# A transformer block with linear attention on one core: the loop over 13 of 17 positions replaced by straight code on all five engines

## The reference

```python
x_norm = (x - mu) * rsqrt(var + EPS) * ln_g + ln_b
q, k, v = split(x_norm @ W_qkv + b_qkv)
gate = sigmoid(x @ W_gate + b_gate); gate = gate / (mean(gate) + EPS)
q = relu(q * gate) ** 2 + EPS;  k = relu(k * gate) ** 2 + EPS
# scan over the rows: kv_s += k_t (x) v_t ; k_s += k_t ; out_t = (q_t . kv_s) / (q_t . k_s + EPS)
x = x + out @ W_proj + b_proj
# feed-forward, on the layer norm of the new x
x = x + gelu((x_n @ U1) @ V1 + b1) @ U2 @ V2 + b2
```

## Time and profile before

| | |
|---|---|
| time, median of 3 runs | 1889.18 us (1887.97 to 1893.83) |
| the profiled execution's own time | 1888.3 us |
| its span, first to last instruction | 1886.3 us |
| mean granted TensorE clock | 0.991 of 2.4 GHz |
| PE busy | 1813.1 us, 96% |
| DVE, POOL, ACT busy | 75%, 47%, 36% |
| instructions recorded | 37376 |

### The profile page before, as it was taken

The page is one execution under the profiler, slowest core; times in us unless marked ns, Lnnn a source line. Parts: engine busy times, 40 slices in busy tenths (PEclk is TensorE's granted clock), DMA queues, the critical chain, the costliest instruction groups (busy, mean ns, idle before and its releaser), DMA issues.

```text
span 1886.3 us, 37376 instructions
## 1 busy us (share of the span) xinstructions
PE 1813.1 (96%) x13753; PEld 1545.6 (82%) x13753; DVE 1407.7 (75%) x2606; ACT 683.7 (36%) x1242; POOL 881.2 (47%) x1091
## 2 busy tenths in 40 slices
PE   6899999999999999999999999999999999999997
PEld 4688888888888888888888888888888888888876
DVE  6777777777777777777777777777777677777775
ACT  4233343343343333333333433433433333333332
POOL 3354554454544545545545444545544455455440
PEclk9999999999999999999999999999999999999999
DMA  6101001001000011010011010010100110100000
GB/s 195 34 18 34 28 31 35 22 25 35 25 33 24 24 35 34 23 35 23 24 34 35 23 34 24 23 35 25 33 24 28 30 34 23 35 23 24 29 18 23
DMA packets 34501, 61.20 MB, mean 32 GB/s; under 512 B 3672, under 2 KB 6256, under 8 KB 34352
## 3 DMA queue, kind: packets, MB, share of 16 engines
q1 hardware_dynamic: 33488, 57.31, 9.6%
q10 hardware_dynamic: 864, 1.57, 0.3%
HBM read 41.96 MB, written 16.91 MB: 31 GB/s over the span
## 4 chain that ended last, share of the span: by engine, by line
issue 36%; POOL 25%; PE 18%; ACT 4%; DVE 3%; POOLq 1%; DVEq 0%
POOL h_lo L372 9%; POOL xs L361 4%; POOL keys L389 3%; POOL small L334 3%; POOL queries L392 2%; PE ps_a L773 2%; PE ps_a L772 2%; PE ps_a L774 2%; POOL key_lo L401 2%; POOL x1s L382 2%; PE ps_b L774 2%; PE ps_b L773 2%; PE ps_b L772 2%; ACT L471 2%; PE ps_q L772 1%
## 5 line engine op out<-in xcount | busy, mean ns | idle before, releaser
L372 POOL TENSOR_TENSOR h_lo<-h_full,h_hi 128x512 fp32r<-128x512 f32 x244 | 313.9, 1286 | 382.8 <-DVE h_hi L602 382.8
L456 ACT ACTIVATE h_full<-ps_h,cols 128x256 f32<-128x256 f32 x512 | 211.1, 472 | 242.7 <-PE ps_h L774 235.2
L602 DVE CAST h_hi<-h_full 128x512 fp32r<-128x512 f32 x256 | 163.6, 639 | 98.8 <-ACT h_full L456 98.7
L772 PE MATMUL ps_b<-wx_hi,zt_hi 128*128 128x512 f32 x512 | 209.7, 410 | 22.7 <-issue 21.5
L334 POOL TENSOR_TENSOR small<-moments,eps_col 128x1 f32<-128x1 f32 x128 | 25.8, 201 | 399.7 <-DVE moments L741 331.7
L772 PE MATMUL ps_a<-wx_hi,zt_hi 128*128 128x512 f32 x512 | 207.2, 405 | 1.3 <-issue 1.2
L774 PE MATMUL ps_b<-wx_hi,zt_lo 128*128 128x512 f32 x512 | 205.4, 401 | 0.0
L773 PE MATMUL ps_b<-wx_lo,zt_hi 128*128 128x512 f32 x512 | 205.3, 401 | 0.0
L774 PE MATMUL ps_a<-wx_hi,zt_lo 128*128 128x512 f32 x512 | 202.2, 395 | 0.0
L773 PE MATMUL ps_a<-wx_lo,zt_hi 128*128 128x512 f32 x512 | 201.8, 394 | 0.0
L772 PE MATMUL ps_q<-h_hi,u_hi 128*128 128x256 f32 x512 | 162.4, 317 | 15.3 <-POOL h_lo L372 9.2
(11 more groups left out here) (160 smaller groups left out, 5052.1 us busy)
## 6 DMA issues: line engine op xcount, KB each, us to landing
xs<-L_attn_x SPq DMA_DIRECT2D x64, 256.0 KB, 2.7
out<-x1s SPq DMA_DIRECT2D x64, 256.0 KB, 2.1
key_sums<-carry_rows SPq DMA_DIRECT2D x60, 256.0 KB, 3.2
x1s<-L_attn_W_qkv SPq DMA_DIRECT2D x8, 256.0 KB, 5.2
x1s<-L_attn_W_gate SPq DMA_DIRECT2D x4, 256.0 KB, 4.0
h_full<-L_attn_W_qkv SPq DMA_DIRECT2D x4, 256.0 KB, 6.3
x1s<-L_ffn_U SPq DMA_DIRECT2D x4, 256.0 KB, 3.6
carry_rows<-key_sums SPq DMA_DIRECT2D x64, 2.0 KB
```

Source lines behind the costliest of these rows:

```text
L372: E.tensor_tensor(h_lo[:, i % 2, :], h_full[:, i % 2, :], h_hi[:, i % 2, :].bitcast(F32), ALU.subtract).then_inc(s["h_lo_ready"], 1)
L456: last = E.activation(h_full[:, i % 2, a * GROUP:(a + 1) * GROUP], ps_h[i % 2][:, a * GROUP:(a + 1) * GROUP], ACT.Gelu_apprx_tanh, bias=b1 ...
L602: E.tensor_copy(h_hi[:, i % 2, :], h_full[:, i % 2, :]).then_inc(s["h_hi_ready"], 1)
L772: E.matmul(ps, wh, mh, start=start and i == 0, stop=False)
```

## The change

The helper steps loses the hardware loop. All 17 positions with their four steps are written out, so p is always a number: the branches are gone from each engine, and with them the register instructions; each wait gets a constant and each DMA a constant row. Order, waits, buffers and the work of a step stay as they are.

```diff
-def steps(eng, step):
-
-    for p in (0, 1):
-        for b in range(4):
-            step(p, b)
-    with eng.Fori(2, POSITIONS - 1) as p:
-        for b in range(4):
-            step(p, b)
-    for p in (POSITIONS - 1, POSITIONS):
-        for b in range(4):
+def steps(step):
+
+    for p in range(POSITIONS + 1):
+        for b in range(BATCHES):
             step(p, b)
...
-            steps(sp, step)
+            steps(step)
...
-            steps(pool, step)
+            steps(step)
...
-            steps(act, step)
+            steps(step)
...
-            steps(dve, step)
+            steps(step)
...
-            steps(pe, step)
+            steps(step)
```

## The result

| | before | after |
|---|---|---|
| time, median of 4 runs | 1888.58 us (1887.96 to 1893.83) | 1856.32 us (1854.23 to 1857.23) |
| ratio, 95% interval | | 0.982 (0.980 to 0.984) |
| the profiled execution | 1888.3 us | 1856.7 us |
| its span | 1886.3 us | 1854.6 us |

The change saves 32 us, 1.8%. The forecast was 1856.0. After it six lines fewer stand at the top, so L772 is now L766, L372 is L366, and L625 is L619.

What follows compares the result with a forecast made beforehand. PE bounds the kernel, held up at its loop's twelve jumps. Span 1886.3 less 32.9 (idle 22.7, restart 3.4, clock 6.2, small shifts 0.6) gives 1853.4, execution 1855.4, raised towards the median to 1856 us; range 1851 to 1866.

Steps and rivals of the forecast that it cites:

- A clean position costs 111.82 us: Positions 2 to 14: a position of straight code without the jump takes 111.82 us, thirteen of them 1453.66 us.
- The difference of 32.9 us goes: Loop of positions 2 to 14: its 1486.60 us exceed thirteen clean positions by 32.9 us, which was expected to go.
- 22.7 us of idle time by "issue": PE at the loop's jumps: 21.5 us in 12 stalls plus 1.2 us in three small stalls behind one would go.
- 6.2 us for the clock: PE behind four of the twelve stalls: the granted clock falls, costing 1.55 us each; without stalls none expected there.
- 3.4 us for the restart: PE around each of 12 stalls: weight loads and matmuls no longer overlap, 0.28 us each, 3.4 us in all.
- Register instructions: All engines in the loop: removing them was costed at nothing; a rival gave up to 7.8 us more gain, chance 0.04.
- the other branches: Loop branches of engines other than PE: 12 x some 50 ns, beside PE's work, costed at nothing.
- Waits for h_lo: PE waiting for POOL's h_lo, about 0.6 us in a position; straight code was not expected to shorten them.
- Block crossings in a row: PE's straight code, some 8 fetch blocks a position: a crossing costed at nothing, bounds 0 and 1.66 to 2.14 us.
- The slower rival, fetch starvation: DVE, ACT, POOL and SP straight code: about 34 more blocks fetched, 3.4 us a miss, up to 1971 us; chance 0.04.
- DVE is next: Without PE's stall DVE is next; its gate waits, 16.0 us in 12 places, go near nothing and nothing becomes late.
- a jump as one fetch of 3.4 us with a cover: PE's loop jump: the branch takes a median 3465 ns, queued matmuls cover part, about half shows as idle time.

Runs made afterwards that it cites:

- small-loop kernel: Full straight code plus, on TensorE behind each of positions 1 to 13, a two-pass loop over one long-met wait: 1856.53 us, ratio 0.985.
- long loop's head moved: TensorE alone loops over two positions a pass, its first instruction now at slot 0 of a 256-instruction block: 1870.09 us, ratio 0.991.
- late-jump loop: Against the kernel before, TensorE alone loops, its jump behind the next position's gate projection: 1915.71 us; with the head at slot 0 of a block 1859.00 us.
- long loop at its first place: TensorE alone loops, over two positions a pass with 6 jumps, head not placed: 1904.32 us, ratio 1.008 to the kernel before.
- the first run: Kernel before with straight code on TensorE alone, the four other engines keeping their loops: 1856.55 us, ratio 0.983.
- the last: Kernel before with all five loops kept, TensorE's branch alone announced at the head of each pass: 1856.31 us, ratio 0.984.
- slot 239: TensorE alone loops as in the kernel before, head placed so that 17 instructions are left in its block: 1908.33 us, ratio 1.013.
- half body: TensorE alone loops, two steps a pass instead of four, 25 jumps, output not the block's: 1856.42 us, ratio 0.985 to the kernel before.

## Why the prediction was right

**A clean position costs 111.82 us.** Measured 111.85 in position 2, and 1454.03 us for 13 of them against 1453.66. Taking the price of straight code from positions that were already written out, and from loop steps without a jump, is what made the forecast good: it needed no price for a branch at all. That the median was hit to 0.3 us is luck. The runs of the changed kernel alone lie 3 us apart, the medians of the kernel before lie between 1883.7 and 1889.2 us, and the sum had given 1855.4 us before it was raised by judgement towards the median.

**The difference of 32.9 us goes.** 32.6 us went in the loop. The start took 1.3 us longer (position 2 begins at 235.29 instead of 234.01), in a part that the change doesn't touch, and the end 0.4 less; hence 31.7 us in the span. The start varies from one execution to the next: between 18.5 and 21.9 us the granted clock was 0.50 in the changed kernel's trace and 1.00 in that of the kernel before. The small-loop kernel, with the same code up to there, shows no such fall at 18.5 us, and its position 2 begins at 233.86 us.

**Its parts.** The 22.7 us of idle time by "issue" are gone to the last row. The rest of the 32.6 us, 9.9 us, is busy time of PE in positions 2 to 14, against 6.2 us for the clock, 3.4 us for the restart and 0.6 us left over in the forecast. How it divides between clock and restart wasn't measured. Over the whole span only 8.1 us of it show, because of the start; I had expected roughly 6 to 8. That a fall of the clock comes with the stall, not with something that straight code has too, is borne out: from position 1 to 15 the granted clock never fell in the changed kernel, nor in any kernel without dear jumps. It fell at 4 of 12 jumps in the kernel before, at 3 of 12 with the loop on TensorE alone, at 2 of 6 with the long loop's head moved, and at each jump of the late-jump loop (second stalls of 2.1 to 3.0 us) and of the long loop at its first place (5.1 to 6.6 us). The long loop at its first place shows the price, with the clock down behind six jumps instead of two: PE busy 1817.9 us against 1805.8 with its head moved. Why the clock falls behind some stalls of 1.7 to 2.2 us and not behind others stays open, as the prediction said.

**Nothing costed at zero cost anything.** Register instructions and the other branches: shown by the first run and the last. Waits for h_lo: 9.2 us before and after. Block crossings in a row: 110 packets on PE's queue, 47 on the other (I had said 48), with no idle time by "issue". The slower rival, fetch starvation, is therefore refuted where it was placed, in straight code: 33 blocks more and no loss. It exists elsewhere, behind VectorE's jump over 556 instructions.

**DVE is next.** It is: its wait for the gate, 16.0 us in 12 places before, has gone from the list, and in positions 2 to 14 the only waits of PE that are left are those for POOL's h_lo (6.9 us, 0.3 us at most).

**Where the reasoning was thin.** The forecast treated a jump as one fetch of 3.4 us with a cover. It didn't matter for straight code, which has no jumps, but it failed at once when I used it for other loops: it missed the second fetch behind a head that lies late in its block, and that a loop whose body the buffer holds can still lose its head. The kernel before had been lucky in its place: with some 37 instructions left in the head's block, the second fetch came just in time in most passes, and late in those three that made up its 1.2 us before ps_a. As to the cover, I took it as ten matmuls. By the trace 10 or 11 matmuls start during a dear branch at the old place and 17 at the later one; why it differs is open. It also called the branches of DVE and POOL near the figure for a compare-and-branch; at 40 to 67 ns they are about half of it, which changes nothing in the sum.

The Trainium skill, in Runtime: NRT & Kernel Launch, section Instruction fetch mechanics, gives TensorE's instruction buffer as 2048 instructions, refilled in blocks of 256. The runs agree: 256 by the stall 17 instructions behind slot 239, and a body of 1812 instructions that stays while one of twice the length doesn't; the 2048 itself no run here tests. The same section says that a taken branch pays where its target isn't in a window of two blocks. The half body of 900 instructions, over three blocks, didn't pay, so on TensorE the measurement decides against the two blocks.

## What to carry to other kernels

If the engine that sets the time shows idle stretches with nothing waited for, count them against the jumps of its loop, and take the price of straight code from passes or steps without a jump; idle time alone understates it (22.7 of 32.6 us here), since the restart and the clock come on top. The cure belongs on that engine alone, and the cheapest is to keep the loop: announce the branch ahead, or shorten the body so that it stays in the buffer (tried here only in a kernel whose output isn't the block's); writing out the other engines' loops brought nothing. Before comparing two loops, look where their heads lie in a fetch block: the place of the head alone moved one loop here by 57 us without changing any work.

## What the runs showed of the hardware that I had not expected

- A loop with dear jumps has a price set by the place of its head: the same loop of two positions took 1904.3 or 1870.1 us, the late-jump loop 1915.7 or 1859.0.
- A branch that is announced leaves the whole body of 1812 instructions in TensorE's buffer: 28 blocks fetched in a run instead of 135.
- On TensorE the fetch shows as the length of the branch (3.4 us); on VectorE the branch stays at 63 ns and the fetch shows as idle time behind it (2.7 us).
- Kernels with dear jumps vary more from run to run (1885.9 to 1896.4 us in ten runs of the loop on TensorE alone) than those without (1854.2 to 1857.8 in all runs of six such kernels).
